# Loop-carried wait values, a loop end moved on TensorE, logits stored earlier, and the r product in two column halves, in a two-layer recurrent kernel

## The chip, the cores and the metric

The kernel runs on one core of one Trainium2 chip. The metric is the device time of one execution in microseconds (us), as a median over runs. The core has five engines with an instruction queue each: TensorE (PE; its weight loads are shown as PEld), VectorE (DVE), ScalarE (ACT), GpSimd (POOL) and SyncE (SP), which here issues the DMAs. The engines wait for each other on semaphores. An instruction waits for a semaphore to reach a constant or to reach the value of a register.

## The reference

Two recurrences of 1024 steps each run one behind the other over 512 sequences (1024 by 64 keys). The inputs are cut to this:

```
# gru: for every t, h is (B, 64)
xp = keys @ Wx + b_in ;  rec = h @ Wh + b_rec
z = sigmoid(xz + rz) ;  r = sigmoid(xr + rr)
hh = relu(xh + r * rh)
h = z * h + (1 - z) * hh                # outs[t]
# attention over time
logit = sum_u outs[t] * (queries @ W_att.T) ;  attn = softmax(logit over t)
# agru: for every t, a = attn[t]
xp = outs @ Wx + b ;  rec = h @ Wh
r = sigmoid(xr + rr) ;  c = relu(xc + r * rc)
h = (1 - a) * h + a * c                 # the last h is the result
```

## The kernel before

**Layout.** The state of all sequences lies as 128 partitions (two halves of the batch with 64 units each) by 256 columns. The columns form two groups, a and b, of 128 columns (GC). The groups are independent, and each engine's queue takes them in turn, so that one group's work covers the other's latency. All matrices are 64 by 64, and each product is made in two halves, one for each half of the partitions.

**Loops.** Each engine runs two hardware loops (`Fori`) of 128 passes. A pass (BODY) is eight time steps, written out. The first loop is the GRU, the second the attention GRU (AGRU); between them lies the softmax. The loop variable t0 counts 0, 8, 16 and so on. Most semaphores go on counting from step to step, and the wait for step s of a pass is on `due = t0 + (s + 2)`. That value is made in a register of the waiting engine by an instruction in its queue, at the place where it is first used. Other semaphores are set back by 8 in each pass by a matmul of PE; waits on these are on constants (`s + 2`).

**One GRU step of one group.** PE adds h times the weights of r (`GH_R`), z (`GH_Z`) and hh (`GH_H`) into banks that hold the product of x and the bias already (L561 for h, L569 for x, L576 for the bias). ACT makes `r_gate` (L358), `z_gate` (L360) and `z_rest` = 1 - z (L361). POOL makes `kept` = z * h (L314) and `prod` (L304), the product for the logits, which PE sums (L623). DVE makes `gated` (L448), adds it up (`vec_bank`, L455), multiplies by `z_rest` (L464) and adds `kept` to give h (L475). Each of these four on DVE is two instructions of 64 columns (`PARTS`). PE starts on h when both halves are there (`h_ready`).

**One AGRU step of one group.** DVE makes `gated` (L519), the candidate (L525) and `a_new` (L532), each one instruction of 128 columns. `state` (L538) follows one group later, behind the other group's `gated`. PE makes the r product of `a_new` (`AH_R`, L561), ACT the sigmoid (L389), and POOL `a_kept` (L331). PE multiplies `a_new` and `a_kept` by the weights apart, so that the product with `a_kept` comes early.

**What DVE's queue holds besides.** In `gru_gated` and `agru_gated`, at s == 0, there is a wait for the r product and a `sem_inc` on `bodies_begun` ahead of the other waits:

```
if s == 0:
    dve.wait_ge(r_summed[g], due)
    dve.sem_inc(bodies_begun, 1)
dve.wait_ge(rh_summed[g], due)
dve.wait_ge(r_ready[g], s + 2)
```

The value of the wait for stores and loads (`stored`, `pairs`) is made from t0 at its first use in a pass, in front of the first h (L474) or the first a_new (L531). The loop's own instructions have the line of the `with` body's last statement in the trace: L478 for DVE's GRU loop and L541 for its AGRU loop.

**PE's second loop.** A pass begins with the r product of `a_new` of group a for step 0, which waits for the last `a_new` of the pass before; the loop's branch and the register instructions of t0 stand right in front of it.

**SP's first loop.** In a pass: x for the next pass, h of the first half out (`store_outs`), x, h of the second half out, and the logits of the last pass out (`store_logits`, two DMAs). ACT copies the next logits at s == 2 (`copy_logits`, L349) and waits there until these two DMAs have landed.

Of the kernel before, what the change touches and what calls it, by code (L numbers as in the profile page):

```python
# [7 lines left out]
ALU = mybir.AluOpType  # L8
# [8 lines left out]
def recurrent_attention_kernel(nc, keys_t, queries_t, weight_columns, bias_columns, agru_b_row, out):  # L17
# [13 lines left out]
    PAIRS, ONES = 32 // BODY, 16 // BODY  # L31
# [8 lines left out]
    with ExitStack() as ctx:  # L40
# [14 lines left out]
        def part_sems(name):  # L55
            return [[sem(f"{name}_{'ab'[g]}{part}") for part, _ in PARTS] for g in GROUPS]

# [53 lines left out]
        r_ready, z_ready, zr_ready = sems("r_ready"), sems("z_ready"), sems("z_rest_ready")  # L111
        gated_ready, cand_ready, new_ready = part_sems("gated_ready"), part_sems("cand_ready"), part_sems("new_ready")
        kept_ready, prod_ready = sems("kept_ready"), sems("prod_ready")
        h_last, x_last, bodies_begun = sems("h_last"), sem("x_last"), sem("bodies_begun")
# [12 lines left out]
        ar_ready, rest_ready = sems("ar_ready"), sem("rest_ready")  # L127
        agated_ready, acand_ready = sems("agated_ready"), sems("acand_ready")

        anew_ready = [[sem(f"anew_ready_{'ab'[g]}{parity}") for parity in range(2)] for g in GROUPS]  # L130
# [6 lines left out]
        FIRST = BODY + 1  # L137

        def seen_by_pe(s, g):

            return s + 2 if g == 0 else (s + 1 if s else FIRST)

# [39 lines left out]
        def _(sp):  # L182
# [152 lines left out]
        def _(act):  # L335
            for g in GROUPS:
                act.sem_inc(z_ready[g], 1)
                act.sem_inc(zr_ready[g], FIRST)
                for q in (r_ready[g], ar_ready[g]):
                    act.sem_inc(q, (1, FIRST)[g])  # L340
# [10 lines left out]
            with act.Fori(0, T, BODY) as t0:  # L351
                for s in range(BODY):
# [3 lines left out]
                    for g in GROUPS:  # L356
                        act.wait_ge(r_summed[g], due)
                        nc.scalar.activation(r_gate[:, g], r_bank[g][:, 0:GC], ACT.Sigmoid).then_inc(r_ready[g], 1)  # L358
# [25 lines left out]
            with act.Fori(0, T, BODY) as t0:  # L384
                for s in range(BODY):
                    done, due = t0 + (s + 1), t0 + (s + 2)
                    for g in GROUPS:
                        act.wait_ge(ar_summed[g], due)
                        nc.scalar.activation(r_gate[:, g], r_bank[g][:, 0:GC], ACT.Sigmoid).then_inc(ar_ready[g], 1)  # L389
# [8 lines left out]
        def _(dve):  # L398
# [26 lines left out]
            for g in GROUPS:  # L425
                for q in (*gated_ready[g], cand_ready[g][0], *new_ready[g], agated_ready[g]):
                    dve.sem_inc(q, 1)
                for q in (cand_ready[g][1], acand_ready[g]):
                    dve.sem_inc(q, FIRST)
                nc.vector.memset(h_at(-1)[:, gcols(g)], 0.0).then_inc(h_ready[g], 1)  # L430
                nc.vector.memset(a_new[:, 1, gcols(g)], 0.0).then_inc(anew_ready[g][1], 1)
                dve.sem_inc(anew_ready[g][1], BODY // 2)
                if g == 1:
                    dve.sem_inc(anew_ready[g][0], BODY // 2)
# [23 lines left out]
            def gru_new(due, s, g):  # L458
                cand, new = vec_parts(g)
                for part, c in PARTS:  # L460
                    dve.wait_ge(cand_ready[g][part], (due, s + 2)[part])
                    if part == 0:
                        dve.wait_ge(zr_ready[g], s + 2)
# [352 lines left out]
```

## Time and profile before

| what | value |
|---|---|
| median of 3 runs | 4429.84 us (4427.02 to 4429.88) |
| the profiled execution | 4430.53 us |
| its span, first to last instruction | 4428.7 us |
| granted TensorE clock, mean | 0.997 |
| PE busy | 4372.4 us, 99% |
| PEld busy | 3968.0 us, 90% |
| DVE busy | 4196.2 us, 95% |
| POOL busy | 2717.1 us, 61% |
| ACT busy | 2286.8 us, 52% |
| instructions | 336421 |

The span is the time from the first to the last instruction of the profiled execution. Busy time counts the overlaps of pipelined instructions of one engine once. Waits, register instructions and branches are not counted as busy. The trace marks them with a q behind the engine (DVEq).

### The profile page before, as it was taken

The page shows a single profiled execution, that of the slowest core. Times are in us where ns is not written, and L with a number is a line of the kernel's source. Part 1 is how long each engine was busy: PE and PEld are TensorE (multiplying, and loading weights), DVE is VectorE, ACT ScalarE, POOL GpSimd, SP SyncE. Part 2 cuts the span into 40 slices and gives each one's busy share as a digit, 9 for nine tenths or more (in the row PEclk, how much of TensorE's full clock was granted, in tenths as well). Part 3 has the DMA queues.
Part 4 walks back from the last instruction along what each step waited for, and adds up shares of the span by engine and source line. Part 5 has one row for each costly group of instructions (what it writes and reads, how often), then busy time and mean ns, then how long its engine had stood idle before and what let it go on. Part 6 is the DMA issues. An engine that isn't in the chain of part 4 may idle for free.

```text
span 4428.7 us, 336421 instructions
## 1 busy us (share of the span) xinstructions
PE 4372.4 (99%) x131196; PEld 3968.0 (90%) x131196; DVE 4196.2 (95%) x24625; ACT 2286.8 (52%) x9363; POOL 2717.1 (61%) x6154
## 2 busy tenths in 40 slices
PE   8999999999999999999998999999999999999999
PEld 7888888888888888888887999999999999999998
DVE  8999999999999999999998999999999999999999
ACT  5666666666666666666654444444444444444444
POOL 6777777777777777777773444444444444444444
PEclk9999999999999999999998999999999999999999
DMA  3333333333333333334334555555555555554554
GB/s 110 115 116 123 115 116 123 115 115 121 117 115 120 119 115 120 119 115 121 118 123 129 129 132 128 128 132 128 128 133 128 128 133 128 128 133 129 127 133 115
DMA packets 169275, 544.13 MB, mean 123 GB/s; under 512 B 31644, under 2 KB 38060, under 8 KB 169260
## 3 DMA queue, kind: packets, MB, share of 16 engines
q1 hardware_dynamic: 169260, 543.93, 44.3%
q8 instruction: 9, 0.15, 0.0%
q14 instruction: 6, 0.05, 0.0%
HBM read 405.24 MB, written 138.56 MB: 123 GB/s over the span
## 4 chain that ended last, share of the span: by engine, by line
DVE 52%; PE 21%; issue 20%; DMA 3%; DVEq 2%; SPq 1%; ACT 0%; ACTq 0%; PEldq 0%
DVE vec_bank L525 12%; DVE gated L448 8%; DVE state L538 7%; DVE a_new L532 6%; DVE vec_bank L455 5%; DVE gated L519 5%; DVE vec_bank L464 5%; DVE h L475 4%; PE r_bank_a L561 4%; PE r_bank_b L561 3%; DMA logits<-logit_rows 2%; PE logit_bank L623 2%; PE z_bank_b L569 2%; PE z_bank_a L569 2%; PE c_bank_a L561 1%
## 5 line engine op out<-in xcount | busy, mean ns | idle before, releaser
L331 POOL TENSOR_TENSOR a_kept<-attn_rest,state 128x128 f32<-128x128 f32 x2048 | 933.6, 456 | 1173.6 <-DVE state L538 1139.0
L314 POOL TENSOR_TENSOR kept<-z_gate,h 128x128 f32<-128x128 f32 x2048 | 933.6, 456 | 533.8 <-ACT z_gate L360 512.0
L304 POOL TENSOR_TENSOR prod<-h,qw 128x128 f32<-128x128 f32 x2050 | 934.6, 456 | 0.0
L569 PE MATMUL r_bank_a<-x,weights 64*64 64x128 f32 x8200 | 881.7, 290 | 12.8 <-ACT r_gate L389 7.1
L569 PE MATMUL r_bank_b<-x,weights 64*64 64x128 f32 x8192 | 892.8, 295 | 0.0
L569 PE MATMUL z_bank_a<-x,weights 64*64 64x128 f32 x8200 | 853.9, 283 | 0.0
L569 PE MATMUL z_bank_b<-x,weights 64*64 64x128 f32 x8192 | 843.3, 283 | 0.0
L623 PE MATMUL logit_bank<-prod,row_sum 64*64 64x128 f32 x8208 | 798.5, 270 | 8.6 <-ACT logit_rows L349 5.0
L464 DVE SCALAR_TENSOR_TENSOR vec_bank<-vec_bank,z_rest 128x64 f32<-128x64 f32 x4096 | 735.9, 225 | 0.4 <-issue 0.3
L475 DVE TENSOR_TENSOR h<-vec_bank,kept 128x64 f32<-128x64 f32 x4096 | 721.3, 218 | 0.0
L389 ACT ACTIVATE r_gate<-r_bank_a 128x128 f32<-128x128 f32 x1024 | 284.0, 277 | 837.5 <-PE r_bank_a L561 837.5
L532 DVE SCALAR_TENSOR_TENSOR a_new<-vec_bank,attn 128x128 f32<-128x128 f32 x2048 | 597.6, 292 | 82.2
L538 DVE TENSOR_TENSOR state<-a_new,a_kept 128x128 f32<-128x128 f32 x2049 | 577.5, 282 | 0.1
L623 PEld LDWEIGHTS logit_bank<-prod,row_sum 64*64 64x64 f32 x8208 | 510.0, 133 | 27.6 <-issue 23.0
L358 ACT ACTIVATE r_gate<-r_bank_a 128x128 f32<-128x128 f32 x1024 | 283.3, 277 | 480.2 <-PE r_bank_a L561 480.2
L358 ACT ACTIVATE r_gate<-r_bank_b 128x128 f32<-128x128 f32 x1024 | 283.8, 277 | 402.9 <-PE r_bank_b L561 402.9
L576 PE MATMUL r_bank_a<-ones,bias_w 64*64 64x128 bf16 x4100 | 471.6, 216 | 0.0
L389 ACT ACTIVATE r_gate<-r_bank_b 128x128 f32<-128x128 f32 x1024 | 283.9, 277 | 352.0 <-PE r_bank_b L561 351.6
L576 PE MATMUL z_bank_a<-ones,bias_w 64*64 64x128 bf16 x4100 | 464.7, 216 | 0.0
L576 PE MATMUL r_bank_b<-ones,bias_w 64*64 64x128 bf16 x4096 | 456.4, 216 | 0.0
L561 PE MATMUL r_bank_a<-h,weights 64*64 64x128 f32 x4096 | 446.4, 294 | 9.7 <-DVE h L475 0.2
L576 PE MATMUL z_bank_b<-ones,bias_w 64*64 64x128 bf16 x4096 | 455.6, 216 | 0.0
(119 smaller groups left out, 17857.4 us busy)
## 6 DMA issues: line engine op xcount, KB each, us to landing
x<-in_keys_t SPq DMA_DIRECT2D x512, 256.0 KB, 3.7
gru_outputs<-h SPq DMA_DIRECT2D x256, 512.0 KB, 2.9
x<-gru_outputs SPq DMA_DIRECT2D x512, 256.0 KB, 3.7
attn<-attention SPq DMA_DIRECT2D x512, 256.0 KB, 3.9
logits<-logit_rows SPq DMA_DIRECT2D x258, 8.0 KB
time_rows<-logits SPq DMA_DIRECT2D x2, 896.0 KB, 7.0
attention<-time_rows SPq DMA_DIRECT2D x2, 896.0 KB, 5.5
weights<-in_weight_columns SPq DMA_DIRECT2D x2, 176.0 KB, 3.7
```

The source lines that it names most:

```text
L304: nc.gpsimd.tensor_tensor(prod[:, (s - 1) % BODY, gcols(g)], h_at(s - 1)[:, gcols(g)], qw[:, gcols(g)], ALU.mult).then_inc(prod_ready[g], 1)
L314: nc.gpsimd.tensor_tensor(kept[:, g], z_gate[:, g], h_at(s - 1)[:, gcols(g)], ALU.mult).then_inc(kept_ready[g], 1)
L331: nc.gpsimd.tensor_tensor(a_kept[:, s % 2, gcols(g)], attn_rest[:, s % 2, gcols(g)], state[:, (s - 1) % 2, gcols(g)], ALU.mult).then_inc(a ...
L389: nc.scalar.activation(r_gate[:, g], r_bank[g][:, 0:GC], ACT.Sigmoid).then_inc(ar_ready[g], 1)
L464: nc.vector.scalar_tensor_tensor(new[:, c], cand[:, c], 0.0, z_rest[:, g, c], ALU.max, ALU.mult).then_inc(new_ready[g][part], 1)
L475: last = nc.vector.tensor_tensor(h_at(s)[:, gcols(g)][:, c], new[:, c], kept[:, g, c], ALU.add)
L532: nc.vector.scalar_tensor_tensor(a_new[:, s % 2, gcols(g)], cand, 0.0, attn_at(s)[:, gcols(g)], ALU.max, ALU.mult).then_inc(anew_ready[g][ ...
L538: nc.vector.tensor_tensor(state[:, s % 2, gcols(g)], a_new[:, s % 2, gcols(g)], a_kept[:, s % 2, gcols(g)], ALU.add).then_inc(s_ready[g], 1)
L561: last = nc.tensor.matmul(dst[lanes(half)], weights[lanes(half), w], moving[lanes(half)], start=start, stop=stop, skip_group_check=True)
L569: last = nc.tensor.matmul(dst[lanes(half)], weights[lanes(1 - half), w], moving[lanes(1 - half)], start=start, stop=False, skip_group_chec ...
L576: last = nc.tensor.matmul(dst[lanes(half)], bias_w[lanes(1 - half), part], ones[lanes(1 - half)], start=False, stop=stop, skip_group_check ...
L623: mm = nc.tensor.matmul(logit_bank[lanes(half), gcols(g)], row_sum[lanes(half), BODY - 1 - i:BODY - 1 - i + U], prod[lanes(half), i, gcols ...
```

## The change

- On DVE the values of the waits stand in two registers that are moved on by 1 in each step (`next_count`) and go on from pass to pass; t0 isn't used. In the GRU the register instruction lies between the candidate and `new` of group b; in the AGRU between the candidate and `a_new` of group b. The value for stores and loads (`filled`) is moved on in the same way, at s == CHUNK.
- The waits at s == 0 with `bodies_begun` are gone. `r_ready` and `ar_ready` become two semaphores for each group, for even and odd steps, and waits on them are on constants.
- PE's registers (`copied`, `loads`, `count`) go on from pass to pass too. PE's second loop is cut at another place: the r product and the c product of `a_new` of group a (`agru_state(0, ...)`) are the end of a pass, where they were its beginning.
- SP stores the logits behind x of the first half, ahead of both h stores.
- In the GRU, r's product with h is made in two halves of 64 columns. The first waits for the first half of h (`h_begun`), the second for the second half (`h_ready`). These are eight matmuls and eight weight loads a step more. The products for z and hh stay whole.

```diff
@@ SP
                     load_x(keys, k + 1, b)
+                    if b == 0:
+                        store_logits(k)
                     store_outs(k, b)
-                store_logits(k)
@@ DVE
             def gru_gated(due, s, g):
-                if s == 0:
-
-                    dve.wait_ge(r_summed[g], due)
-                    dve.sem_inc(bodies_begun, 1)
                 dve.wait_ge(rh_summed[g], due)
-                dve.wait_ge(r_ready[g], s + 2)
+                dve.wait_ge(r_ready[g][s % 2], by_parity(s))
...
-                    last = nc.vector.tensor_tensor(h_at(s)[:, gcols(g)][:, c], new[:, c], kept[:, g, c], ALU.add)
-                last.then_inc(h_ready[g], 1)
-
-            with dve.Fori(0, T, BODY) as t0:
-                stored = t0 * ONES + 16
+                    nc.vector.tensor_tensor(h_at(s)[:, gcols(g)][:, c], new[:, c], kept[:, g, c],
+                                            ALU.add).then_inc((h_begun, h_ready)[part][g], 1)
+            def next_count(s):
+                dve.reg_add(counts[(s + 1) % 2], counts[s % 2], 1)
+
+            dve.reg_mov(counts[0], 2)
+            dve.reg_mov(filled, 16)
+            with dve.Fori(0, T, BODY):
                 for s in range(BODY):
-                    due = t0 + (s + 2)
+                    due = counts[s % 2]
                     for g in GROUPS:
                         gru_gated(due, s, g)
                         gru_cand(due, s, g)
+                        if g == 1:
+                            next_count(s)
                         gru_new(due, s, g)
-                        gru_h(due, stored, s, g)
+                        gru_h(due, filled, s, g)
+                        if g == 0 and s == CHUNK:
+                            dve.reg_add(filled, filled, 16)
...
             def agru_gated(due, s, g):
-                if s == 0:
-
-                    dve.wait_ge(ar_summed[g], due)
-                    dve.sem_inc(bodies_begun, 1)
-                dve.wait_ge(ar_ready[g], s + 2)
+                dve.wait_ge(ar_ready[g][s % 2], by_parity(s))
                 dve.wait_ge(rc_summed[g], due)
...
+            with dve.Fori(0, T, BODY):
                 for s in range(BODY):
-                    due = t0 + (s + 2)
+                    due, done = counts[s % 2], counts[(s + 1) % 2]
                     agru_gated(due, s, 0)
                     agru_sum(done, s - 1, 1)
                     agru_cand(due, s, 0)
-                    agru_new(due, pairs, s, 0)
+                    agru_new(due, filled, s, 0)
                     agru_gated(due, s, 1)
                     agru_sum(due, s, 0)
                     agru_cand(due, s, 1)
-                    agru_new(due, pairs, s, 1)
-                    done = due
+                    if s == CHUNK:
+                        dve.reg_add(filled, filled, 32)
+                    next_count(s)
+                    agru_new(due, filled, s, 1)
@@ PE, first loop
-                        pe.wait_ge(h_ready[g], s + 1)
-                        own(r_bank[g][:, 0:GC], GH_R, hs, False, True).then_inc(r_summed[g], 1)
+                        for part, c in PARTS:
+                            pe.wait_ge((h_begun, h_ready)[part][g], s + 1)
+                            last = own(r_bank[g][:, c], GH_R, hs[:, c], False, True)
+                        last.then_inc(r_summed[g], 1)
@@ PE, second loop
-            with pe.Fori(0, T, BODY) as t0:
-                soon = count(0, t0, 1)
...
+            agru_state(0, 0, 0)
+            with pe.Fori(0, T, BODY):
                 for s in range(BODY):
+                    agru_ahead(0, s, s)
+                    pe.reg_add(count[(s + 1) % 2], count[s % 2], 1)
+                    agru_state(1, s, s + 1)
+                    agru_ahead(1, s, s + 1)
+                    agru_state(0, (s + 1) % BODY, s + 1 if s < BODY - 1 else 0)
```

`agru_state(g, ...)` is the two products of `a_new` of group g with the x product of r of the other group between them, and `agru_ahead(g, ...)` is everything that the old body made behind these for the other group (the products of `a_kept`, and the x product of c). In its order on PE nothing else differs.

## Rows read from the trace of the kernel before

**Rows 1.** The page's first line.
```profile
span 4428.7 us, 336421 instructions
```

**Rows 2.** Sources L518, L478, L541: op, count, min/median/max ns, first and last start us.
```profile
L518 DVEq ALU_OP  x896: 40/40/47, 2355.1 to 4424.1; - x180
...
L478 DVEq ALU_OP  x128: 40/40/40, 34.5 to 2317.1; - x128
...
L541 DVEq ALU_OP  x128: 40/40/40, 2369.3 to 4425.8; - x128
```

**Rows 3.** Timeline of DVE, GRU: start us, us of the pair, engine, line.
```profile
1994.08 0.35 DVE L448 TENSOR_TENSOR gated<-c_bank_a,r_gate 128x64 f32<-128x64 f32 x2 [0.42 <-PE c_bank_a L561]
...
2005.01 0.36 DVE L448 TENSOR_TENSOR gated<-c_bank_a,r_gate 128x64 f32<-128x64 f32 x2
...
2006.08 0.35 DVE L448 TENSOR_TENSOR gated<-c_bank_b,r_gate 128x64 f32<-128x64 f32 x2
...
2007.17 0.36 DVE L448 TENSOR_TENSOR gated<-c_bank_a,r_gate 128x64 f32<-128x64 f32 x2
```

**Rows 4.** Chain of waits over a loop end, GRU: start us, us, what.
```profile
2011.18 0.18 DVE h L475
...
2011.67 0.05 DVEq L478
...
2011.77 0.02 DVEq L444
...
2011.89 0.02 DVEq L446
...
2011.96 0.23 DVE gated L448
```

**Rows 5.** Chain of waits behind it, GRU, first h of the pass.
```profile
2012.76 0.05 DVEq L474
```

**Rows 6.** Waits, whole span: us in total, times, longest us.
```profile
ACT logit_rows L349 <- DMA logits<-logit_rows: 39.0, 110, 4.9
```

**Rows 7.** Timeline of DVE, AGRU, one step.
```profile
3025.64 0.29 DVE L519 TENSOR_TENSOR gated<-c_bank_a,r_gate 128x128 f32<-128x128 f32 x1
...
3026.37 0.29 DVE L532 SCALAR_TENSOR_TENSOR a_new<-vec_bank,attn 128x128 f32<-128x128 f32 x1
3026.58 0.28 DVE L519 TENSOR_TENSOR gated<-c_bank_b,r_gate 128x128 f32<-128x128 f32 x1
...
3027.30 0.29 DVE L532 SCALAR_TENSOR_TENSOR a_new<-vec_bank,attn 128x128 f32<-128x128 f32 x1
3027.59 0.29 DVE L519 TENSOR_TENSOR gated<-c_bank_a,r_gate 128x128 f32<-128x128 f32 x1
```

**Rows 8.** Timeline of ACT, the same step.
```profile
3026.17 0.28 ACT L389 ACTIVATE r_gate<-r_bank_b 128x128 f32<-128x128 f32 x1 [0.35 <-PE r_bank_b L561]
3027.20 0.28 ACT L389 ACTIVATE r_gate<-r_bank_a 128x128 f32<-128x128 f32 x1 [0.75 <-PE r_bank_a L561]
```

**Rows 9.** Timeline of PE, the same step.
```profile
3027.53 0.28 PE L561 MATMUL r_bank_b<-a_kept,weights 64*64 64x128 f32 x2
...
3027.65 0.33 PE L561 MATMUL r_bank_b<-a_new,weights 64*64 64x128 f32 x2
```

**Rows 10.** Chain of waits over a loop end, AGRU.
```profile
3033.19 0.05 DVE a_new L532
...
3033.59 0.05 DVEq L541
...
3033.88 0.07 DVE gated L519
```

**Rows 11.** Timeline of PE, GRU, one group's products of h.
```profile
2007.28 0.33 PE L561 MATMUL r_bank_b<-h,weights 64*64 64x128 f32 x2
...
2007.44 0.28 PE L561 MATMUL r_bank_b<-h,weights 64*64 64x128 f32 x2
...
2007.55 0.28 PE L561 MATMUL z_bank_b<-h,weights 64*64 64x128 f32 x2
```

More of the change, by code:

```diff
@@ L56, in part_sems, with parity_sems @@
             return [[sem(f"{name}_{'ab'[g]}{part}") for part, _ in PARTS] for g in GROUPS]
+        def parity_sems(name):
+            return [[sem(f"{name}_{'ab'[g]}_{('even', 'odd')[parity]}") for parity in range(2)] for g in GROUPS]
         weights = sb("weights", [P, 11, U])
@@ L473, in gru_h @@
                         if g == 0 and s % CHUNK == 0:
[L474 to L479 removed]
+                            dve.wait_ge(outs_stored[s // CHUNK % 2], stored)
+                    nc.vector.tensor_tensor(h_at(s)[:, gcols(g)][:, c], new[:, c], kept[:, g, c],
+                                            ALU.add).then_inc((h_begun, h_ready)[part][g], 1)
+            counts = [dve.alloc_register(f"dve_count_{i}") for i in range(2)]
+            filled = dve.alloc_register("dve_filled")
+            def next_count(s):
[3 more added lines that the diff above has]
+            with dve.Fori(0, T, BODY):
                 for s in range(BODY):
[L481 removed]
+                    due = counts[s % 2]
                     for g in GROUPS:
@@ L539, in agru_sum @@
                                         a_kept[:, s % 2, gcols(g)], ALU.add).then_inc(s_ready[g], 1)
-            with dve.Fori(0, T, BODY) as t0:
-                pairs = t0 * PAIRS + 32
-                done = t0 + 1
+            dve.reg_mov(counts[0], 2)
+            dve.reg_mov(counts[1], 1)
+            dve.reg_mov(filled, 32)
+            with dve.Fori(0, T, BODY):
                 for s in range(BODY):
-                    due = t0 + (s + 2)
+                    due, done = counts[s % 2], counts[(s + 1) % 2]
                     agru_gated(due, s, 0)
@@ L586, in _ @@
             counts = [pe.alloc_register(f"pe_count_{i}") for i in range(4)]
-            def count(i, base, more):
-                pe.reg_add(counts[i], base, more)
-                return counts[i]
             pe.wait_ge(w_loaded, 16 * N_WEIGHT_DMAS)
@@ new lines, in _, with agru_state @@
+            count, loads = counts[:2], counts[2:]
+            def agru_state(g, s, n):
+                ns = a_new[:, (s - 1) % 2, gcols(g)]
+                o = 1 - g
+                pe.wait_ge(anew_ready[g][(s - 1) % 2], ANEW[s - 1])
+                own(r_bank[g][:, 0:GC], AH_R, ns, False, True).then_inc(ar_summed[g], 1)
+                pe.wait_ge(ar_ready[o][(n - 1) % 2], by_parity(n - 1))
+                if g == 1 and n % CHUNK == 0:
+                    b = n // CHUNK % 2
+                    pe.wait_ge(x_loaded[b], loads[b])
+                    pe.reg_add(loads[b], loads[b], 32)
+                agru_x_r(o, n, (acand_ready[g], -BODY) if s == 0 else None)
+                own(hid_part(g), AH_C, ns, False, True).then_inc(rc_summed[g], 1)
@@ new lines, in agru_ahead @@
+            def agru_ahead(g, s, n):
+                o = 1 - g
+                alone()
+                pe.wait_ge(agated_ready[o], count[n % 2])
+                pe.wait_ge(akept_ready[o], count[n % 2])
+                last = own(hid_part(o), AH_C, from_kept(o, n), True, False)
+                seen = (n - 2) % BODY
+                if seen in (BODY - 2, BODY - 1):
+                    last.then_inc(anew_ready[o][seen % 2], -HALF)
+                pe.wait_ge(axr_summed[o], n + 1)
+                last = own(r_bank[o][:, 0:GC], AH_R, from_kept(o, n), False, False)
+                if (n - 1) % BODY >= BODY - 2:
+                    last.then_inc(ar_ready[o][(n - 1) % 2], -HALF)
+                pe.wait_ge(acand_ready[o], seen_by_pe(s, o))
+                agru_x_c(o, n, (x_used, CHUNK) if g == 0 and s % CHUNK == CHUNK - 1 else None,
+                         (axr_summed[o], -BODY) if s == BODY - 1 else None)
@@ new lines, in _ @@
+            pe.reg_mov(count[0], 1)
+            pe.reg_mov(loads[1], 32 * (BODIES + 1))
+            pe.reg_mov(loads[0], 32 * (BODIES + 3))
+            agru_state(0, 0, 0)
+            with pe.Fori(0, T, BODY):
+                for s in range(BODY):
+                    agru_ahead(0, s, s)
[3 more added lines that the diff above has]
+                    agru_state(0, (s + 1) % BODY, s + 1 if s < BODY - 1 else 0)
```

100 lines of the change are left out of this document (42 added, 58 removed).

## The prediction

> **What bounds the kernel now.** I read the page first. PE is 99% busy, but a span of 4428.7 us [rows 1] is not thereby PE's: its busy time counts pipelined matmuls from start to modelled end, while the chain that ended last lies on DVE for half of the span and on PE for a fifth. So I went by stages, in the timelines of one pass of each loop.
>
> In the GRU, DVE's instructions follow each other without a hole: a half step of one group is four pairs of 64-column instructions, and gated of a, b, a start at 2005.01, 2006.08 and 2007.17 [rows 3]. A step is 2.16 us, of which only about 0.04 is anything but DVE's own queue. PE starts on h the moment it is there: one product of h is two passes per half of the array; the first pass of r starts 0.16 us before the second, later ones 0.11 apart [rows 11]. Per half step the queue has eight such passes (r, z, hh, logits), 8 x 0.11 + 0.05 = 0.93 us, against a half step of 1.08: PE has some 0.15 to spare.
>
> In the AGRU a step is 3027.59 - 3025.64 = 1.95 us [rows 7], and here DVE does have a hole. From a_new of a to gated of b it is 0.21 us (3026.37 to 3026.58), DVE's own pace. From a_new of b to gated of a it is 0.29 (3027.30 to 3027.59). That gated waits for ACT's r_gate of a, which runs from 3027.20 for 0.28, so to 3027.48 [rows 8]; gated starts 0.11 later. r_gate of b ends at 3026.45, 0.13 before its gated, and binds nothing. Between r_gate's end and gated of a lies the register instruction (40 ns, 896 times, seven in each of 128 passes, source L518 [rows 2]) that makes `due` and, being first in the queue, carries the wait for r_gate.
>
> At the loop ends, DVE needs from its last h (2011.18, a pair's second instruction) to the next gated 0.78 us [rows 4], where the next instruction of a pair otherwise comes after about 0.14. In the AGRU it is 0.69 (3033.19 to 3033.88) [rows 10] instead of 0.29.
>
> **The change, part by part.** All sums are against the profiled execution (4430.5 us; 0.7 above the median of the runs).
>
> *GRU, DVE's loop end.* The loop's own instructions give the mean pass: (2317.1 - 34.5)/127 = 17.97 us [rows 2]; the pass shown is 2011.96 - 1994.08 = 17.88 [rows 3, 4]. Removed: one of the two register instructions of t0 at the loop end, 2011.67 to the next at 2011.77, 0.10; the wait for the r product with its increment, 2011.77 to 2011.89, 0.12 [rows 4]. The branch stays. Sum 0.22, all on the path, since nothing of PE or ACT binds there: gated of the new pass would have been ready. Also removed: the register instruction of `stored` in front of the first h [rows 5], of the same kind as the one for 0.10, so 0.10. Added: one plain register instruction for `filled`, 0.03 (the 40 ns one partly beside the running instruction); bounds 0 and 0.08. The per-step register instruction is moved from in front of gated a to between cand and new of b, in a queue that is equally full in both places: 0, bounds +0.04 and -0.04 (if it costs DVE nothing behind a running instruction). Sum: 0.22 + 0.10 - 0.03 = 0.29 a pass.
>
> *GRU, the logits' store.* ACT waits for it 39.0 us in all, 110 times, up to 4.9 [rows 6]. What of this reaches DVE is at most the difference between the mean pass and the pass shown, 17.97 - 17.88 = 0.09 a pass, 11.5 us in all. The two DMAs, issued before the store of the first half of h instead of after both, land several steps earlier, so I take 0.08 of the 0.09; bounds 0 and 0.09. The h stores are passed by two small DMAs (8 KB each, against 512 KB) in SP's queue; the wait of the first h for `outs_stored` has half a pass of cover, so 0.
>
> *GRU, r's product in two halves.* Adds four 64-column passes and takes off two of 128 per half step. Their columns are the same. The first half starts about 0.1 us earlier, because h's second instruction is no longer waited for, and r is ready earlier; but DVE does not wait for r, so this buys 0. It costs 0 if a 64-column pass takes half of 0.11 and its weight load stays beside it: the one load that shows (0.16 - 0.11 = 0.05 [rows 11]) just fits beside 0.055. Bounds of a 64-column pass: 0.055, and 0.11 if the load sets the pace (then a half step needs 4 x 0.11 + 6 x 0.11 = 1.10, 0.02 over now); 0.16 if nothing overlaps. I take 0.055, nearest to the loads' 0.05 steps.
>
> GRU: (0.29 + 0.08) x 128 = 47 us.
>
> *AGRU, DVE.* With the register instruction away from r_gate's end, the delay from r_gate to gated of a falls from 0.11 towards a plain hand-over. Its bounds: 0.03 from one DVE instruction to the next and 0.11, as now. The gain is bounded also by DVE's floor: both a_new-to-gated distances 0.21 make a step of 1.95 - 0.08 = 1.87. I take that, 0.08 in each of the seven steps which have the instruction, 0.56 a pass. PE's order must follow: its r product with `a_kept` for b starts its second pass at 3027.53 and is 0.11 long, and the product with a_new starts at 3027.65 [rows 9], so at this spot PE has no slack, and the other half step has what is in excess of 0.93: 1.95 - 0.93 = 1.02. A step of 2 x 0.93 = 1.86 is the least that PE allows: just under 1.87. Loop end: again 0.10 for t0 and 0.12 for the wait and its increment, 0.22 of the 0.29 that lie between 3033.59 and 3033.88 [rows 10], the rest being the last wait and the first instruction's start; the register instruction of `pairs` in front of the first a_new 0.10; added `filled` 0.03 and, at the loop's first step, the per-step instruction, now hidden behind cand. Sum 0.56 + 0.22 + 0.10 - 0.03 = 0.85; the mean pass is (4425.8 - 2369.3)/127 = 16.19 [rows 2]. I take 0.86, as step 0 gets a little of the hand-over too: 110 us.
>
> *PE's loop ends.* PE's branch now follows the c product of a_new of a, where its next instruction is the product with `a_kept` of b. That one gets 0.08 to 0.13 later, in a stretch in which b has about 0.16 in hand (r_gate of b ends 0.13 before its use [rows 7, 8]): 0, bounds 0 and 0.05 a pass (6 us). In exchange the r product of a, on DVE's shortest path, no longer stands behind the branch; without this part the gain at DVE's loop end would wait for PE.
>
> Sum: 47 + 110 = 157, so 4430.5 - 157 = 4273.
>
> **A rule weighed.** The row says that only the first weight load of a product shows, 0.05 us [rows 11]. The Trainium skill ("TensorE: Matmul & The Clock Gate", Part 3, The mechanism) says that a weight load overlaps with running matmuls only when it goes to another row group; r's four passes per half go to the same rows. By this rule the split would pay for its loads; by the row it pays nothing. The rows 0.11 apart for 128 columns show no load between passes on the same rows, so they speak against the rule here; what it would do is rival B.
>
> **The rivals.**
> A. *The register instruction was never the delay.* 0.11 after r_gate's end is what ACT to DVE takes, and the next instruction's own wait takes the place. For it: 21 ns waits are followed by 0.04 to 0.07 at the loop ends too [rows 4, 10]. Against: b's gated never shows 0.11. The AGRU then loses 0.56 x 128 = 72 of its gain: 4345; with half of it, 4309. Beside it: the Trainium skill ("Perfetto Trace Analysis") has DVE's sequencer run ahead of instructions that stand in a wait queue, which would make a register instruction free where it isn't the one that waits.
> B. *PE becomes the bound in the GRU* through unhidden loads: half step 1.10 to 1.12 instead of 1.08, +0.04 to 0.08 on 1024 steps, 40 to 80 us: 4313 to 4353.
> C. *The other side.* The same mechanism at a higher price: a 64-column pass at 0.16 makes the half step 4 x 0.16 + 6 x 0.11 = 1.30, 0.22 over now, +0.44 a step: 4273 + 450 = 4723. It decides once the half step is over 1.08 + 157/2048 = 1.157, that is a 64-column pass over 0.125. Against: no row shows more than one bare load of 0.05.
> D. *The change doesn't do it*: the loop ends keep their length, because something else (PE's branch, ACT's t0) ends there last, and r_gate's hand-over is as in A: only `stored`, `pairs` and the logits stay, 0.10 + 0.10 + 0.08 less 0.06, 28 us: 4402; with nothing at all within 0.2% (9 us), about what a measurement of this kernel can tell from no change.
> E. *More than forecast*: DVE's moved register instructions cost nothing behind a long instruction, GRU step 2.12: -38, 4235.
>
> **How the numbers follow.** Chances: the forecast 0.60 (4250 to 4300), A 0.14, B 0.09, C 0.05, D 0.06 (half of it within 0.2%), E 0.06. The range leaves out C, D and little else: 4225 to 4360. Slower by over 0.2% 0.05, within 0.03, faster 0.92. The likeliest case's own range is 4250 to 4300.
>
> **What the profile after would show.** AGRU: a_new of b to gated of a 0.21 and a step of 1.87; the register instruction no longer in front of gated; loop end 0.47. GRU: step still 2.15, loop end 0.56, no wait for the logits' store on ACT, 8192 matmuls more, passes of r 0.055 apart. The GRU's loop lasts about 2.25 ms, the AGRU's 1.95. Wrong: an r_gate-to-gated delay still at 0.11 (A), PE passes of r at 0.11 or more with gaps on DVE in front of gated (B, C), a wait for PE at the first gated of a pass (D).

## The result, and the profile after

| what | before | after |
|---|---|---|
| median, runs on the same chip | 4428.43 us | 4310.33 us (4309.05 to 4311.54) |
| ratio, 95% interval | | 0.9733, 0.9716 to 0.975 |
| span of the profiled execution | 4428.7 us | 4308.4 us |
| GRU, first gated of group a to the last pass's last | 2298.9 us | 2267.4 us |
| AGRU, the same | 2071.5 us | 1983.2 us |

The kernel is 118 us faster; the forecast was 157 us, at 4273. The profile has 120 us of it: 31.5 in the GRU and 88.3 in the AGRU, where 47 and 110 were forecast. The page after, its first lines and the chain by line, which answers to [rows 1]:

```profile
span 4308.4 us, 353483 instructions
...
PE 4270.3 (99%) x139402; PEld 4086.6 (95%) x139402; DVE 4131.9 (96%) x24625; ACT 2330.6 (54%) x9363; POOL 2719.7 (63%) x6154
...
PE 99%; DVE 1%; DMA 0%; issue 0%; SPq 0%; ACT 0%; ACTq 0%; DVEq 0%; PEldq 0%
```

The 8206 further matmuls are there (131196 before). The chain now runs over PE for 99% of the span, where it lay on DVE for 52% before. That isn't to be read as "PE bounds": PE's records join end to end, and a chain that steps back from one to the next never leaves them. The distances on DVE below, and two experiments that change DVE's queue alone (one took 51 us off, one added 51), say what sets the pace.

The timeline of DVE in the AGRU, two steps in a row; it answers to [rows 7]:

```profile
3317.56 0.29 DVE L546 SCALAR_TENSOR_TENSOR a_new<-vec_bank,attn 128x128 f32<-128x128 f32 x1
3317.77 0.29 DVE L533 TENSOR_TENSOR gated<-c_bank_a,r_gate 128x128 f32<-128x128 f32 x1
...
3318.50 0.29 DVE L546 SCALAR_TENSOR_TENSOR a_new<-vec_bank,attn 128x128 f32<-128x128 f32 x1
3318.71 0.28 DVE L533 TENSOR_TENSOR gated<-c_bank_b,r_gate 128x128 f32<-128x128 f32 x1
...
3319.43 0.29 DVE L546 SCALAR_TENSOR_TENSOR a_new<-vec_bank,attn 128x128 f32<-128x128 f32 x1
3319.64 0.29 DVE L533 TENSOR_TENSOR gated<-c_bank_a,r_gate 128x128 f32<-128x128 f32 x1
...
3320.37 0.29 DVE L546 SCALAR_TENSOR_TENSOR a_new<-vec_bank,attn 128x128 f32<-128x128 f32 x1
3320.74 0.29 DVE L533 TENSOR_TENSOR gated<-c_bank_b,r_gate 128x128 f32<-128x128 f32 x1
```

The reader is to see two things. The step is 3319.64 - 3317.77 = 1.87 us as forecast, and from a_new of b to gated of a it is 0.21 us, no longer 0.29. But in the step that begins at 3319.64 (number 3 of the pass, counted from 0) a_new of a to gated of b is 0.37 instead of 0.21. The timeline of ACT in front of it, which answers to [rows 8]: r_gate of a ends at 3319.61, 0.03 before its gated.

```profile
3319.33 0.28 ACT L398 ACTIVATE r_gate<-r_bank_a 128x128 f32<-128x128 f32 x1 [0.67 <-PE r_bank_a L578]
```

The AGRU's loop end in DVE's timeline is 3329.52 - 3329.03 = 0.49 us (0.69 before [rows 10]):

```profile
3329.03 0.29 DVE L546 SCALAR_TENSOR_TENSOR a_new<-vec_bank,attn 128x128 f32<-128x128 f32 x1
3329.52 0.29 DVE L533 TENSOR_TENSOR gated<-c_bank_a,r_gate 128x128 f32<-128x128 f32 x1 [0.19 <-issue]
```

The GRU's loop end, and the first step behind it, in the same view (0.57 from the start of the last pair of h to gated; 0.78 before, [rows 4]):

```profile
2002.19 0.35 DVE L481 TENSOR_TENSOR h<-vec_bank,kept 128x64 f32<-128x64 f32 x2
2002.76 0.36 DVE L454 TENSOR_TENSOR gated<-c_bank_a,r_gate 128x64 f32<-128x64 f32 x2 [0.22 <-issue]
...
2004.09 0.35 DVE L461 TENSOR_TENSOR vec_bank<-c_bank_b,gated 128x64 f32<-128x64 f32 x2
2004.50 0.36 DVE L470 SCALAR_TENSOR_TENSOR vec_bank<-vec_bank,z_rest 128x64 f32<-128x64 f32 x2
```

Between the starts of the last two pairs there are 0.41 us, where in the other steps the same two pairs are 0.29 apart, and the trace names no wait.

One pass step by step shows where the time went. Each number is the median over the passes of the distance in us between the starts of gated of group a in one step and the next; the last column adds up a loop's distances, means included. "Moved" and "both" are kernels of the experiments.

| loop, kernel | 0 | 1 | 2 | 3 | 4 | 5 | 6 | 7 | sum |
|---|---|---|---|---|---|---|---|---|---|
| GRU before | 2.316 | 2.164 (mean 2.239) | 2.156 | 2.156 | 2.156 | 2.156 | 2.156 | 2.638 | 2298.9 |
| GRU after | 2.281 | 2.148 | 2.146 | 2.146 | 2.182 | 2.148 | 2.202 | 2.452 | 2267.4 |
| GRU moved | 2.158 | 2.148 | 2.146 | 2.148 | 2.183 | 2.147 | 2.146 | 2.471 | 2246.3 |
| AGRU before | 2.058 | 1.960 | 1.962 | 1.962 | 1.962 | 1.963 | 1.962 | 2.362 | 2071.5 |
| AGRU after | 1.874 | 1.871 | 1.871 | 2.042 | 1.871 | 1.871 | 1.871 | 2.222 | 1983.2 |
| AGRU moved | 1.874 | 1.873 | 1.873 | 1.944 | 1.873 | 1.871 | 1.873 | 2.074 | 1952.9 |
| AGRU both | 1.874 | 1.874 | 1.873 | 1.871 | 1.872 | 1.872 | 1.872 | 2.004 | 1934.7 |

Three entries of "after" were not forecast: the AGRU's step 3 (0.17 over the others), the GRU's step 6 (0.055 over) and step 0, which fell by 0.035 only. The experiments are about these, and about which part of the change earned what.

### The profile page after: what moved, and what is told of

It reads as the page before. It is cut to its first block, busy times and chain, and to the rows that moved or that the text cites. A ratio compares the mean times of both kernels' runs of the same rounds, so it can differ in the third digit from the quotient of the medians.

```text
span 4308.4 us, 353483 instructions
## 1 busy us (share of the span) xinstructions
PE 4270.3 (99%) x139402; PEld 4086.6 (95%) x139402; DVE 4131.9 (96%) x24625; ACT 2330.6 (54%) x9363; POOL 2719.7 (63%) x6154
## 4 chain that ended last, share of the span: by engine, by line
PE 99%; DVE 1%; DMA 0%; issue 0%; SPq 0%; ACT 0%; ACTq 0%; DVEq 0%; PEldq 0%
PE r_bank_b L578 14%; PE r_bank_a L578 14%; PE c_bank_a L578 12%; PE c_bank_b L578 11%; PE logit_bank L636 8%; PE z_bank_b L586 7%; PE z_bank_a L586 6%; PE r_bank_a L586 4%; PE z_bank_a L578 4%; PE z_bank_b L578 4%; PE r_bank_b L586 3%; PE c_bank_a L593 3%; PE c_bank_b L593 2%; PE c_bank_a L586 2%; PE c_bank_b L586 2%; PE z_bank_a L593 1%
## 5 line engine op out<-in xcount | busy, mean ns | idle before, releaser
L586 PE MATMUL r_bank_a<-x,weights 64*64 64x128 f32 x8200 | 893.7, 292 | 12.5 <-ACT r_gate L398 6.9
L586 PE MATMUL r_bank_b<-x,weights 64*64 64x128 f32 x8196 | 881.7, 292 | 0.0
L578 PE MATMUL r_bank_b<-h,weights 64*64 64x64 f32 x8192 | 474.7, 234 | 1.8 <-issue 1.8
L578 PE MATMUL r_bank_a<-h,weights 64*64 64x64 f32 x8192 | 473.8, 234 | 0.1
```

The costliest lines, as they stand in the source:

```text
L578: last = nc.tensor.matmul(dst[lanes(half)], weights[lanes(half), w], moving[lanes(half)], start=start, stop=stop, skip_group_check=True)
L586: last = nc.tensor.matmul(dst[lanes(half)], weights[lanes(1 - half), w], moving[lanes(1 - half)], start=start, stop=False, skip_group_chec ...
```

## The experiments

**TensorE's register addition.** Steps 3 and 7 of the AGRU are those in which TensorE waits for a new x and adds to that wait's register behind it (L787, 256 times). Two stretches of PE's timeline of the changed kernel, the same products of b in step 2 and in step 3:

```profile
3317.90 0.33 PE L578 MATMUL r_bank_b<-a_new,weights 64*64 64x128 f32 x2
3317.91 0.33 PE L586 MATMUL r_bank_a<-x,weights 64*64 64x128 f32 x2
...
3319.78 0.44 PE L578 MATMUL r_bank_b<-a_new,weights 64*64 64x128 f32 x4
3319.98 0.33 PE L586 MATMUL r_bank_a<-x,weights 64*64 64x128 f32 x2
```

The x product starts 0.01 us behind the r product in step 2 and 0.20 behind it in step 3. The semaphore event at the end of the c product that is queued behind comes 0.815 us after gated of a in the ordinary steps and 0.909 in steps 3 and 7. In the kernel before, which has the wait without the addition, the x product is 0.10 late in the same two steps and that event is not (0.728, as in the steps beside them).

```diff
@@ agru_state
                     pe.wait_ge(x_loaded[b], loads[b])
-                    pe.reg_add(loads[b], loads[b], 32)
@@ TensorE, ahead of its second loop
-            pe.reg_mov(loads[1], 32 * (BODIES + 1))
-            pe.reg_mov(loads[0], 32 * (BODIES + 3))
+            pe.reg_mov(loads[1], 32 * BODIES)
+            pe.reg_mov(loads[0], 32 * (BODIES + 2))
@@ the loop
                     pe.reg_add(count[(s + 1) % 2], count[s % 2], 1)
+                    if (s + 1) % CHUNK == 0:
+                        b = (s + 1) // CHUNK % 2
+                        pe.reg_add(loads[b], loads[b], 32)
```

> The changed kernel with one edit on TensorE: in the AGRU the register addition for the x loads, which follows the wait for x in steps 4 and 8 of a pass, is moved to the place of the per-step count, a step ahead. Theory 1 (that addition holds up the c product of group b, whose end comes 0.094 us later at these two steps than at the others, and the gated of b behind it): the end comes at 0.81 us from gated of a again instead of 0.91, step 3 loses about 0.09 and step 7 about 0.06 us, 0.15 a pass, 128 passes, about 20 us less: 4290. Theory 2 (the wait for x alone is what costs; the addition is free): no change, 4310.

Measured: 4289.19 us, ratio 0.969 (0.9674 to 0.9706). Step 3 is 1.948 and step 7 is 2.150, 0.094 and 0.072 less. In PE's timeline of this kernel the x product is 0.11 late:

```profile
3309.25 0.33 PE L578 MATMUL r_bank_b<-a_new,weights 64*64 64x128 f32 x2
3309.36 0.33 PE L586 MATMUL r_bank_a<-x,weights 64*64 64x128 f32 x2
```

The first theory holds: the addition alone cost 21 us, 0.07 to 0.09 each time, though it lasts 32 ns itself. It stood in the middle of PE's queue, in front of products that DVE waits for.

**VectorE's code, moved.** What stays of step 3 is 0.075, and in the GRU 0.125 in step 0 and 0.055 in step 6. At these places DVE's next instruction comes late with nothing to wait for that the trace shows. Counted through DVE's records from its first, which is number 0, the three late ones are number 63 and number 191 (18th and 146th of the first loop, which begins at 46) and number 319 (55th of the second, which begins at 265): 128 apart each time. The kernel before has a late one at number 63 too (0.058), but none at its number 191 (GRU, step 6, 2.156) nor at 319 (AGRU, step 3, 1.962). So such a place is late in some kernels only. The test: other instructions ahead of the first loop.

```diff
+            for _ in range(56):
+                dve.reg_mov(counts[1], 2)
             dve.reg_mov(counts[0], 2)
             dve.reg_mov(filled, 16)
```

> The changed kernel with 56 register moves put in front of VectorE's first loop, each without effect. Theory 1 (VectorE's queue stalls for 0.05 to 0.12 us where its code crosses a fixed grid of 128 instructions: in the changed kernel instructions 63, 191 and 319 of the engine): the first loop starts at instruction 102 and has one crossing, at its 90th instruction, the second starts at 321, ends at 444 and has none. The stalls at the 18th and 146th instruction (0.125 and 0.055 us a pass) give way to one of 0.05 to 0.12, that at the 55th of the AGRU (0.10) is gone: 0.16 to 0.23 us a pass, 20 to 29 us, less some 2 us for the moves at the start: 4285 to 4292. Theory 2 (these stalls belong to the operations around them, waits that the profile does not name): they stay where they are, 4310 to 4313.

Measured: 4310.66 us (0.9738, 0.9721 to 0.9754), nothing moved. This is no verdict: the moves, each overwritten by the next, are not in the trace, and the loop still begins at number 46. The run that joined it to the first experiment therefore says the same as that one:

> Both edits together. If both first theories hold and add up: 4310 - 20 - 20 = 4270, at the lower end 4262. If only one of them holds: 4285 to 4292. If neither: 4310.

Measured: 4289.47 us (0.9689, 0.9672 to 0.9705). With increments of a spare semaphore, which stay in the queue:

```diff
+        spare = sem("spare")
...
+            for _ in range(56):
+                dve.sem_inc(spare, 1)
             dve.reg_mov(counts[0], 2)
```

> The 56 register moves of the run before this one never reached the queue (the first loop still began at VectorE's 46th instruction), so that run said nothing on the grid. Here 56 increments of a spare semaphore stand there instead, which nothing waits for. Theory 1 (the queue stalls where its code crosses every 128th instruction, at 63, 191, 319): the first loop starts at 102, the stalls of 0.125 and 0.055 us at its 18th and 146th instruction are gone and one shows at the 90th, the second loop starts at 321 and that of 0.10 us at its 55th is gone: 20 to 29 us less, 2 to 3 more at the start: 4284 to 4293. Theory 2 (the stalls belong to these operations or to their distance from the loop's start): they stay, 4310 to 4313.

Measured: 4259.59 us, ratio 0.9616 (0.9599 to 0.9632), 51 us less than the changed kernel: more than either theory gave. The table's rows "moved" have it: the GRU's step 0 loses 0.123 and its step 6 0.056; its new crossing, the 90th instruction, costs nothing that can be seen. The AGRU's step 3 loses 0.098. Together that is 0.277 a pass, or 35 us, of which the GRU's step 7 gives 2 back; the first theory had forecast 20 to 29, with a new delay at the 90th instruction. It holds against the second, for no operation of a loop and no distance within one has changed. The rest is in the AGRU's step 7 with its loop end, 0.148 in 128 passes or 19 us, which the theory did not have. DVE's timeline of this kernel, the loop end of a pass:

```profile
3292.86 0.29 DVE L549 SCALAR_TENSOR_TENSOR a_new<-vec_bank,attn 128x128 f32<-128x128 f32 x1
3293.20 0.29 DVE L536 TENSOR_TENSOR gated<-c_bank_a,r_gate 128x128 f32<-128x128 f32 x1
```

0.34 us, where the changed kernel has 0.49. DVE's branch lasts 0.056 in both, but the next instruction starts 0.19 us after the branch's start instead of 0.33. What has changed for this branch is where its loop lies: 124 instructions from number 321 to 444, between the lines of the grid at 319 and 447, where they went from 265 to 388 over the line at 319. The GRU's loop has 187 instructions and always crosses a line; its branch did not get shorter (0.29, and 0.31 moved). Only one displacement was tried in each kernel, so a grid of 128 is what fits all these places, and no other distance was tested against it.

Can it be that the code is loaded anew in every pass? The page after lists the DMA loads of instructions (queue, kind: packets, MB, share), for all engines together:

```profile
q8 instruction: 10, 0.16, 0.0%
q14 instruction: 6, 0.05, 0.0%
```

These are 16 packets in the whole execution, against 256 passes of the two loops, and none of them lies between 60 and 2200 us or between 2400 and 4200 us, in the changed kernel or in the moved one. A load by DMA in every pass is out. What the queue does at these places instead stays open.

To see whether this belongs to the change or to any kernel of this kind, the kernel before with 62 such increments, so that its second loop lies between the same two lines:

```diff
+            for _ in range(62):
+                dve.sem_inc(spare, 1)
             with dve.Fori(0, T, BODY) as t0:
                 stored = t0 * ONES + 16
```

> The kernel before with 62 increments of a spare semaphore in front of VectorE's first loop, so that its second loop (120 instructions from the 322nd on) lies between two lines of the grid of 128, as in the changed kernel moved by 56. Theory 1 (the second loop's branch goes back to code that VectorE's queue still holds, which in the changed kernel took 0.14 us off each loop end): about 0.13 off the AGRU's loop end and 0.05 to 0.06 off the stall in the GRU's first step, 128 passes: 23 to 25 us less, 4405. The change is then worth 4405 - 4260 = 145 us between kernels whose code lies alike. Theory 2 (the gain of 51 us needs the changed kernel): 4430.

Measured: 4409.58 us, ratio 0.9958 (0.9942 to 0.9973). The AGRU's last step went from 2.362 to 2.237 (0.125), the GRU's first from 2.316 to 2.252 (0.064), while the GRU's steps 1 and 7 each got a little longer (0.03 and 0.02 in the mean), so that of the 19 us most is in the AGRU (15.1 in the profile, against 2.6 in the GRU). The first theory holds: the kernel before had paid for the place of its code as well. Between kernels that lie alike the change is worth 4409.6 - 4259.6 = 150 us, give or take the 2 us by which the kernel before differed beside the two.

**Both edits together**, TensorE's addition and the 56 increments:

> The changed kernel with both edits that gained: the register addition of TensorE moved (20 us by itself) and VectorE's code moved by 56 instructions (51 us by itself). If they are independent: steps 3 and 7 of the AGRU, 1.944 and 2.074 us in the run with the code moved, lose 0.07 and 0.06, 17 us: 4242. If they were the same time seen twice: 4260.

Measured: 4241.80 us (4240.26 to 4242.18), ratio 0.9579 (0.9566 to 0.9592). The two gains add up but for 3 us: 68.5 together, 21.1 and 50.7 apart. This is the fastest of the kernels here. The AGRU's steps are all 1.87, but for the loop end's 2.00; DVE's timeline has gated of a, for instance, at

```profile
3275.33 0.29 DVE L536 TENSOR_TENSOR gated<-c_bank_a,r_gate 128x128 f32<-128x128 f32 x1
...
3277.20 0.29 DVE L536 TENSOR_TENSOR gated<-c_bank_a,r_gate 128x128 f32<-128x128 f32 x1
...
3279.07 0.29 DVE L536 TENSOR_TENSOR gated<-c_bank_a,r_gate 128x128 f32<-128x128 f32 x1
...
3280.95 0.29 DVE L536 TENSOR_TENSOR gated<-c_bank_a,r_gate 128x128 f32<-128x128 f32 x1
```

**The register instruction at gated of a.** Two runs put the per-step addition of DVE's second loop back to group a. First in front of all waits of gated:

```diff
-                    next_count(s)
                     agru_new(due, filled, s, 1)
+                    next_count(s)
```

> The changed kernel with the per-step register addition of VectorE in the AGRU put behind a_new of group b, in front of gated of group a of the next step, as it was before. The prediction's theory (a register instruction there delays gated of a from about 0.04 to 0.11 us behind r_gate): steps of 1.871 go back to about 1.95, 0.08 in seven or eight steps of 128 passes, 72 to 82 us more: 4382 to 4392. Rival A of the prediction (the delay was the hand-over itself, and something else in the change made the step short): 4310.

Measured: 4311.61 us (0.974, 0.9724 to 0.9757): the theory missed as I had written it, a register instruction there costs nothing. The steps stay at 1.873, with 0.21 from a_new of b to gated of a in DVE's timeline:

```profile
3319.89 0.29 DVE L546 SCALAR_TENSOR_TENSOR a_new<-vec_bank,attn 128x128 f32<-128x128 f32 x1
3320.10 0.29 DVE L533 TENSOR_TENSOR gated<-c_bank_a,r_gate 128x128 f32<-128x128 f32 x1
```

But this is not what the kernel before did. There the addition stood between two waits of gated:

```diff
                 dve.wait_ge(ar_ready[g][s % 2], by_parity(s))
+                if g == 0:
+                    dve.reg_add(due, counts[(s + 1) % 2], 1)
                 dve.wait_ge(rc_summed[g], due)
...
-                    next_count(s)
                     agru_new(due, filled, s, 1)
```

> The run with the register addition in front of gated of group a cost nothing: there it ran before the wait for r_gate and was done long before. In the kernel before, it stood between that wait and the wait for the c product, and so carried the first of them. This run puts it there in the changed kernel, in every step. Theory 1 (a register instruction costs where it stands behind the last wait to end): it starts after r_gate is there, steps of 1.871 become about 1.95, 0.08 to 0.09 in eight steps of 128 passes: 82 to 92 us more, 4392 to 4402. Theory 2 (rival A: the hand-over takes 0.11 only in the timing of the kernel before): 4310.

Measured: 4361.59 us, ratio 0.9847 (0.9831 to 0.9863), 51 us more. The addition's row (L533) and DVE's timeline of the run, with 0.30 from a_new of b to gated of a:

```profile
L533 DVEq ALU_OP  x1024: 40/40/40, 2318.8 to 4352.8; - x171
```

```profile
3339.98 0.29 DVE L535 TENSOR_TENSOR gated<-c_bank_a,r_gate 128x128 f32<-128x128 f32 x1
...
3341.64 0.29 DVE L548 SCALAR_TENSOR_TENSOR a_new<-vec_bank,attn 128x128 f32<-128x128 f32 x1
3341.94 0.29 DVE L535 TENSOR_TENSOR gated<-c_bank_a,r_gate 128x128 f32<-128x128 f32 x1
```

The first seven steps of a pass are 1.960 or 1.961 again. The 51 us are less than the 82 forecast because steps 3 and 7, at 2.042 and 2.222 in the changed kernel, had room for it (they became 1.960 and 2.170). Rival A is out: the delay was the instruction, and it costs where it stands behind the wait that ends last.

**r's product in one piece.** In PE's timeline of the changed kernel r's product of one group (a pass of 64 columns for each x2) and z's behind it:

```profile
2006.10 0.33 PE L578 MATMUL r_bank_a<-h,weights 64*64 64x64 f32 x4
2006.25 0.33 PE L586 MATMUL r_bank_b<-x,weights 64*64 64x128 f32 x2
2006.27 0.30 PE L578 MATMUL r_bank_a<-h,weights 64*64 64x64 f32 x4
2006.40 0.28 PE L578 MATMUL z_bank_a<-h,weights 64*64 64x128 f32 x2
```

From the first pass to z's it is 0.30 us, where it was 0.27 [rows 11]. The run undoes the split:

```diff
-                        for part, c in PARTS:
-                            pe.wait_ge((h_begun, h_ready)[part][g], s + 1)
-                            last = own(r_bank[g][:, c], GH_R, hs[:, c], False, True)
-                        last.then_inc(r_summed[g], 1)
+                        pe.wait_ge(h_ready[g], s + 1)
+                        own(r_bank[g][:, 0:GC], GH_R, hs, False, True).then_inc(r_summed[g], 1)
```

> The changed kernel with r's product of h in one piece, behind h_ready, as before. The prediction's theory (VectorE binds the GRU, r is not waited for): no difference, 4308 to 4313; the GRU's step stays at 2.147 us. Rival B (the passes of 64 columns cost TensorE more than half of one, and hold the step): faster, by up to 0.04 in six steps, 30 us: 4280. A third theory (the earlier r is what took the step from 2.156 to 2.147 us): slower by 0.009 x 1024 = 9 us or more: 4320.

Measured: 4315.15 us, ratio 0.9742 (0.9726 to 0.9758), an interval that holds the changed kernel's 0.9733. The profile is sharper: the GRU took 2270.0 us instead of 2267.4, its ordinary steps 2.154 to 2.156 instead of 2.146 to 2.148. So the split earns about 0.008 in each of five steps of a pass, 3 to 5 us in all. That is the third theory at about half its size, and not the prediction's "no difference"; rival B is out.

**TensorE's loop end**, twice, once in the changed kernel and once in the one with both edits:

```diff
-            agru_state(0, 0, 0)
             with pe.Fori(0, T, BODY):
                 for s in range(BODY):
+                    agru_state(0, s, s)
                     agru_ahead(0, s, s)
...
                     agru_ahead(1, s, s + 1)
-                    agru_state(0, (s + 1) % BODY, s + 1 if s < BODY - 1 else 0)
```

> The changed kernel with TensorE's second loop cut where it was: the two products of a_new of group a at the head of a pass, behind the branch. The prediction's theory: the r product of a then comes up to 0.17 us late at the loop end, and VectorE's gated with it: 0.05 to 0.15 us more in each of 128 passes, 6 to 20 us: 4317 to 4330. Rival (the loop end is VectorE's own branch, TensorE's lies beside it): 4310.

> The kernel with both edits, and TensorE's second loop cut where it was before the change. In the changed kernel that cost nothing. Theory 1 (VectorE's branch alone hid it; now that it is 0.14 us shorter, the r product of group a comes last at the loop end): 0.05 to 0.14 us in each of 128 passes, 6 to 18 us more than the kernel with both edits: 4248 to 4260. Theory 2 (TensorE's loop end is not on the path at all): the same, 4242.

Measured: 4311.07 us (0.973, 0.9714 to 0.9746) and 4243.40 us (0.9584, 0.957 to 0.9599), 0.7 and 1.6 us more than their counterparts. The first is within what the runs scatter; in the second all four runs lie above the five of the counterpart (4243.07 to 4245.37 against 4240.26 to 4242.18). So where TensorE's loop ends is worth 2 us at most, and the first theory of both texts (6 to 20 us, 6 to 18 us) missed.

**The logits first**, in the kernel before:

```diff
                     load_x(keys, k + 1, b)
+                    if b == 0:
+                        store_logits(k)
                     store_outs(k, b)
-                store_logits(k)
```

> The kernel before with one edit on SyncE: the store of the logits ahead of the first store of h. The prediction's term: 0.08 us in each of 128 passes, 10 us less: 4420; step 1 of the GRU 2.156 us in the mean too instead of 2.239. Rival (hidden already, or the h stores come late instead): 4430.

Measured: 4420.27 us, ratio 0.9982 (0.9973 to 0.9991), 8 us less. Step 1 of the GRU is 2.156 in the mean as in the median, and the GRU's loop 9.9 us shorter. In the changed kernel ACT's wait for this store, 39.0 us in 110 times before [rows 6], is 4.9 us, once.

## Why the prediction came out as it did

Range and sign held; the size was 39 us too large, and the likeliest case's own range, 4250 to 4300, was missed by 10 us. The time alone would have spoken for rival A at half its size (4309), which the run with the addition between the two waits rules out. By its steps:

- *AGRU, the hand-over from r_gate.* Right: 0.21 from a_new of b to gated of a, steps of 1.871 against 1.87 forecast, and the two runs with the addition put back say that it was this instruction. The price was 0.09 a step, not 0.08. The one step that shows none of it, step 3, lost it to two terms below.
- *AGRU, loop end and `pairs`.* Right: 0.69 to 0.49 at the loop end (0.22 forecast), and step 0 lost 0.184 (0.10 and 0.08 forecast).
- *GRU, loop end.* 0.186 instead of 0.22, 24 us instead of 28. The two instructions are gone from the trace, but from the branch to the next instruction it is now 0.29 instead of 0.27. No run undoes this edit alone; its share is read from the traces. The prediction also misread a row here, without use in its sum: 2011.18 is where the last pair of h starts, not the pair's second instruction, from which it is 0.64 to the next gated.
- *GRU, "the register instruction of `stored` in front of the first h" [rows 5].* Forecast 0.10, and step 0 fell by 0.035 only. The term itself was right: from the instruction before it to the first h it was 0.222 and is 0.131, 0.09 less. What failed is that the sum took the rest of the step as unchanged: the late one at DVE's number 63, which cost 0.058 in the kernel before, grew to 0.125.
- *Logits' store.* Right: 0.083 in step 1, by itself 8 to 10 us.
- *`filled`.* 0.035 in the GRU's step 4 against 0.03.
- *GRU, the per-step register instruction.* Forecast 0 for the move, and so it was: in front of gated of a it had made the next start 0.157 apart instead of 0.131, and between candidate and `new` of b it makes it 0.154. In this full queue it costs about 0.02 in either place; it is not free, as rival E had it.
- *r's product in halves.* Forecast 0, measured 3 to 5 us gained. PE begins 0.05 us behind the first half of h and has it all done in time.
- *PE's loop ends.* Forecast 0 of cost, which held. But the sentence that without this part the gain at DVE's loop end would wait for PE was wrong: two runs show that it would not, but for 2 us at most.
- *What the sum left out.* TensorE's register additions had no term, and no reason stood for that. `loads` in the AGRU, 256 additions of 32 ns, cost 21 us. The prediction said of such an instruction on DVE what it does in a queue, and didn't ask the same of PE, whose old loop made these values at its head.
- *What no row of the kernel before gave a price for.* The place of the code: a new late instruction in the GRU's step 6 (0.055), one in the AGRU's step 3 (0.098) and the growth in step 0 (0.07), together 0.22 a pass or 28 us. Against it stand some 14 us that the ordinary steps gained more than forecast (0.011 in seven of the AGRU, 0.008 in four of the GRU, 128 passes). The loop ends gave 7 us less than forecast (0.034 and 0.02 a pass), and the two delays in step 3 overlap by 3 us (0.094 and 0.098 one by one, 0.171 together). 157 - 21 - 28 + 14 - 7 + 3 = 118, of 120 in the profile. That the gap was only 39 us is in part luck: some 56 us of missed costs stand against 17 of missed gains. Between kernels whose code lies alike the change brought 150.

## What to carry to other kernels

A register instruction costs by its place in the queue. In front of waits in which the engine stands idle it was free here. Behind the wait that ends last, or between two products that another engine waits for, it put up to 0.09 us on the path, more than the 32 to 40 ns that it lasts. Look for it on every engine that the edit touches. When a change alters the number of instructions of an engine's loop, its time contains where the code now lies; compare such kernels with some instructions put ahead of the loop. If the forecast's steps all measure as forecast and the sum doesn't, go through one pass step by step: the entries that differ from their neighbours are the missing terms.

## What the runs showed of the hardware

- In the changed kernel DVE's next instruction comes 0.055 to 0.125 us late where its queue crosses number 63, 191 and 319, counted from 0 at the engine's first in the trace, each 128 behind the other; 56 instructions put ahead took all three delays away. Not every such crossing is late: the kernel before is late at 63 and not at 191 or 319, and the moved one not at 191. What decides is open.
- From the start of the loop's branch, which lasts 0.056 us itself, to the next instruction it is 0.27 to 0.33 us when the loop lies over such a line and 0.19 to 0.20 when it lies between two (the AGRU's loops of the moved kernels). DMA loads of instructions, 16 in all, lie outside the stretches of 60 to 2200 and 2400 to 4200 us, so neither is a load by DMA in each pass; the cause stays open.
- The Trainium skill ("Advanced Engine Details and Errata", ISA Cache) gives the engines' instruction cache, but for TensorE's, two lines of 256 instructions each. The same section calls the size configurable for each engine. The distance measured here is 128 instructions, and whether it is that cache's line no run shows. The same page (Control Flow Timing) has a compare-and-branch at about 108 ns; here the record is 0.056 us long, and it was 0.19 to 0.33 us to the next instruction.
- A matmul product of 64 columns took PE half the time of one of 128 but for the first pass of each half: in the changed kernel's records the four passes of r and the one behind start 0.107, 0.058, 0.075 and 0.058 us apart, 0.298 in all against 0.27 for the two passes of 128 [rows 11]. The Trainium skill's rule on weight loads of the same row group ("TensorE: Matmul & The Clock Gate", Part 3, The mechanism) would have had each of the four pay for its load; beyond the 0.05 in front of the second pass, which the passes of 128 show too [rows 11], at most 0.02 a pass shows. So the trace disagrees with that rule. The same section also lets a load into the background weight buffer go ahead of running matmuls; that would fit, and no run here tells which buffer was loaded.
